# Two attention layers and a post-norm attention in one program: tables made in the first stage, the next weights split inside its last sequence, no wait for the last rows between stages, and the first stage's norm on ScalarE

## What is computed

```python
# stage 1: causal attention, 16 heads of 16, on x [8, 512, 256]; all biases are inputs
q, k, v = split_heads(x @ w_qkv + b_qkv)
a = softmax((q k^T + causal_mask) / sqrt(16))
z = a v
y = z @ w_out + b_out                 # then x + y, normed over its 256 columns
# stage 2, two layers: local attention (8 heads of 64, window 128, l2-normed and rotated q, k), then a gated FFN
for layer in range(2):
    h = shift_token(x); q, k, v = h @ wqkv
    x = x + local_attention(rot(l2norm(q)), rot(l2norm(k)), v) @ wo
    h = layernorm(shift_token(x)) * lg + lb
    a, g = split(h @ w1 + b1)
    x = x + (a * gelu(g)) @ w2 + b2
```

## Time and profile before

| what | value |
| --- | --- |
| median of 3 runs | 2063.98 us (2062.27 to 2068.06) |
| the profiled execution's own time | 2061.79 us |
| its span in the profile | 2060.3 us |
| mean granted TensorE clock | 0.922 of 2.4 GHz |
| TensorE, VectorE, ScalarE, GpSimd busy | 88%, 55%, 46%, 46% of the span |
| first attention | from 7.6 to about 564.9 us |
| local 0 | to 1068.8 us |
| feed-forward 0 | to 1292.7 us |
| local 1 | to 1798.7 us |
| feed-forward 1 | to the end |

### The profile page before, as it was taken

How to read it: one execution, slowest core, us unless ns; L and a number is a source line. 1 busy time by engine, 2 the same in 40 slices (tenths; PEclk the granted TensorE clock), 3 DMA queues, 4 the chain that set the end, 5 groups by cost and what they waited for, 6 DMA issues and landing times. The chain is left out here.

```text
span 2060.3 us, 41179 instructions
## 1 busy us (share of the span) xinstructions
PE 1815.2 (88%) x13304; PEld 1348.1 (65%) x13304; DVE 1141.5 (55%) x2885; ACT 941.3 (46%) x1834; POOL 940.9 (46%) x926
## 2 busy tenths in 40 slices
PE   4899988889569999999969999599999999798887
PEld 2556555655346777777758888467777777577676
DVE  3566665656367766766523333766676666333343
ACT  2555555655335554455434444255445555333322
POOL 3355444554435555554433333355554545333433
PEclk8899888987679999999979999799999999889998
DMA  4333343332210000000111112100000000221221
GB/s 124 107 114 102 102 128 106 120 112 62 72 32 12 31 31 31 31 31 20 48 56 41 61 61 92 43 11 31 31 31 31 31 20 4 79 72 51 81 71 41
DMA packets 103655, 121.27 MB, mean 59 GB/s; under 512 B 23290, under 2 KB 75700, under 8 KB 103604
## 3 DMA queue, kind: packets, MB, share of 16 engines
q1 hardware_dynamic: 96692, 95.45, 15.3%
q0 software_dynamic: 6912, 25.17, 3.3%
HBM read 82.55 MB, written 37.77 MB: 58 GB/s over the span
## 5 line engine op out<-in xcount | busy, mean ns | idle before, releaser
L425 DVE TENSOR_REDUCE a_negm<-a_x 128x2 f32<-128x256 f32 (+3 forms) x256 | 202.5, 815 | 142.1 <-PE a_x L539 139.7
L804 POOL TENSOR_TENSOR work<-work 128x512 f32<-128x512 f32 x128 | 164.7, 1286 | 196.8 <-DVE work L953 195.6
L394 ACT ACTIVATE a_PT<-a_c 128x384 f32<-128x384 f32 (+1 forms) x384 | 184.1, 523 | 138.7 <-PE a_c L578 87.3
L971 DVE CUSTOM_DVE_ANT_0 l_x<-l_x,window 128x256 f32<-128x256 f32 (+1 forms) x512 | 184.4, 422 | 44.7 <-PE l_x L1067 44.0
L1462 DVE SCALAR_TENSOR_TENSOR m_hid<-m_a,mw_b,m_gate 128x512 f32<-128x512 f32 x96 | 71.9, 749 | 246.8 <-ACT m_gate L1401 222.7
L1001 PE MATMUL l_f<-w_hi,tails 128*128 128x512 f32 x384 | 174.9, 455 | 15.0 <-DVE work L953 11.9
L1359 POOL TENSOR_TENSOR m_hid_lo<-m_hid,m_hid_hi 128x512 fp32r<-128x512 f32 x80 | 102.8, 1294 | 134.6 <-ACT m_hid_hi L1412 134.4
L882 ACT ACTIVATE l_PT<-l_c 128x512 f32<-128x512 f32 (+1 forms) x256 | 124.7, 539 | 79.0 <-PE l_c L1103 79.0
L1002 PE MATMUL l_f<-w_hi,tails 128*128 128x512 f32 x384 | 155.3, 405 | 0.0
L1003 PE MATMUL l_f<-w_lo,tails 128*128 128x512 f32 x384 | 154.6, 403 | 0.0
L818 POOL TENSOR_TENSOR l_PS<-l_PT 128x768 f32<-128x768 f32 x64 | 119.7, 1871 | 76.0 <-ACT l_PT L882 76.0
(11 more groups left out here) (238 smaller groups left out, 5115.6 us busy)
## 6 DMA issues: line engine op xcount, KB each, us to landing
a_Q<-qk_parts SPq DMA_DIRECT2D x192, 64.0 KB, 2.1
a_K<-qk_parts SPq DMA_DIRECT2D x192, 64.0 KB, 2.1
qk_parts<-a_qk_hi SPq DMA_DIRECT2D x32, 256.0 KB, 2.1
qk_parts<-a_qk_lo SPq DMA_DIRECT2D x32, 256.0 KB, 2.1
after_attn<-l_out POOLq DMA_DIRECT2D x16, 512.0 KB, 5.8
xin<-after_attn SPq DMA_DIRECT2D x32, 256.0 KB, 3.1
m_xr<-after_attn SPq DMA_DIRECT2D x16, 512.0 KB, 4.1
xin<-in_L_attn_x SPq DMA_DIRECT2D x8, 512.0 KB, 3.5
```

Of the source, the lines that this page charges most:

```text
L394: nc.scalar.activation(PT[:, p // PG % 2, 2 * (p % PG) + hh, QOFF[t]:QOFF[t] + nq], SC[hh][:, 0:nq], ACT.Exp, scale=AD ** -0.5).then_inc(e ...
L425: dve.tensor_reduce(negm[:, q, 2 * p:2 * p + 2], MX[i % 2][:, :, 0:nk], AX.X, ALU.max, negate=True).then_inc(max_done, 1)
L804: pool.tensor_tensor(t1[:, par, w, :], t1[:, par, w, :], t2[:, par, w, :], ALU.add)\
L971: m = dve.tensor_tensor_reduce(out=o, in0=o, in1=mask, scale=-1.0, scalar=-NEG, op0=ALU.add, op1=ALU.min, accum_out=negm[:, q + t, p // 2, ...
```

## The change

1. The constant tables are made at the head of GpSimd's list in `first_attention` (`make_constants`), and the zero rows are set by VectorE there and stored by SyncE in the last sequence. The two blocks ahead of the first attention are gone.
2. At the start, the weights come in two halves with a semaphore each, the four bias columns in two transfers, and the splits of the weights stand behind those of the rows (`f_xe`) on ScalarE and VectorE. `wo_hi` is made after `f_qe:3`, `wo_lo` before `f_sm:4`.
3. In the last sequence of the first attention, SyncE loads the next weights at the first step, ScalarE makes the three high parts after `st:12`, `st:18` and `z3:1`, VectorE the three low parts after `ms:5`, `z0:2` and `z2:3`.
4. The row norm of the first attention (step `end`) runs on ScalarE as scale and bias per row; GpSimd computes the negated mean times the root beside the root, and stores.
5. Stages share one tile `rows_out`. The wait for the eight stores at the end of a stage is gone (but for the last stage); the next stage waits for them (`own.ready`) before it loads sequence 1 or later, before the residual load and before it writes `rows_out`.

The core of the diff:

```diff
+def make_constants(pool, k):
+
+    made = k["made"]
+    pool.memset(k["ident"][:, :], 0.0).then_inc(made, 1)
+    pool.wait_ge(made, 1)
+    pool.affine_select(out=k["ident"][:, :], in_=k["ident"][:, :], compare_op=ALU.not_equal, fill=1.0, base=0,
+                       pattern=[[-1, P]], channel_multiplier=1).then_inc(made, 1)
...
+        HIGH, LOW = [("st", 12), ("st", 18), ("z3", 1)], [("ms", 5), ("z0", 2), ("z2", 3)]
+        FIRST_OF_LAST = [s for s in STEPS if s[0][0] != "f"][0]
...
-                sp.dma_start(w_raw[:, :, :], w_qkv.rearrange("(k p) n -> p k n", p=P)).then_inc(w_loaded, 16)
-                for m, c in enumerate((0, DM, P, DM + P)):
-                    sp.dma_start(bqk[:, m:m + 1], b_qkv[c:c + P].unsqueeze(1),
-                                 allow_slow_non_contiguous=True).then_inc(w_loaded, 16)
+                for k in range(KT):
+                    sp.dma_start(w_raw[:, k, :], w_qkv[P * k:P * k + P]).then_inc(w_loaded[k], 16)
+                for n in range(2):
+                    sp.dma_start(bqk[:, n::2], b_qkv[DM * n:DM * n + DM].rearrange("(h p) -> p h", p=P),
+                                 allow_slow_non_contiguous=True).then_inc(b_loaded, 16)
...
-                steps(sp, do)
-                sp.wait_ge(parts_out, NB * 128)
-                sp.wait_ge(lo_done, NB * 4)
-                ahead.load(sp, ahead_raw, ahead_wo)
-                sp.wait_ge(front_full, NB * NF)
-                sp.wait_ge(stored, 16)
-                ahead.first(sp)
+                def tail(name, i):
+                    if (name, i) == FIRST_OF_LAST:
+                        sp.wait_ge(parts_out, NB * 128)
+                        sp.wait_ge(lo_done, NB * 4)
+                        ahead.load(sp, ahead_raw, ahead_wo)
+                        zeros.store(sp)
+                        sp.wait_ge(front_full, NB * NF)
+                        sp.wait_ge(stored, 16)
+                        ahead.first(sp)
...
                         pool.tensor_scalar(ve[:, :], mv[:, :, 1], LN_EPS, None, ALU.add).then_inc(rstd_a, 1)
-                        pool.wait_ge(rstd_a, b + 2)
+                        pool.tensor_scalar(nb[:, :], mv[:, :, 0], -1.0, None, ALU.mult).then_inc(rstd_a, 1)
+                        pool.wait_ge(rstd_a, 2 * b + 3)
                         pool.tensor_tensor(rs[:, :], ve[:, :], half[:, :], ALU.pow).then_inc(rstd_done, 1)
+                        pool.wait_ge(rstd_done, 2 * b + 1)
+                        pool.tensor_tensor(nb[:, :], nb[:, :], rs[:, :], ALU.mult).then_inc(rstd_done, 1)
                     elif name == "end":
-                        wait_apart(pool, K, rstd_done, b + 1)
-                        wait_apart(pool, K, stored, b * 16)
-                        for t in range(TB):
-                            pool.tensor_scalar(out[:, t, :], y[:, t, :], mv[:, t, 0:1], rs[:, t:t + 1],
-                                               ALU.subtract, ALU.mult).then_inc(out_done, 1)
-                        pool.wait_ge(out_done, b * TB + TB)
+                        wait_apart(pool, K, out_done, b * TB + TB)
                         pool.dma_start(dst[b, 1:1 + S].rearrange("(t p) d -> p t d", p=P),
                                        out[:, :, :]).then_inc(stored, 16)
 
                 steps(pool, do)
-                pool.wait_ge(stored, 16 * NB)
...
+                    elif name == "end":
+                        act.wait_ge(rstd_done, 2 * b + 2)
+                        act.wait_ge(stored, b * 16)
+                        for t in range(TB):
+                            nc.scalar.activation(out[:, t, :], y[:, t, :], ACT.Identity, scale=rs[:, t:t + 1],
+                                                 bias=nb[:, t:t + 1]).then_inc(out_done, 1)
...
+                def tail(name, i):
+
+                    if (name, i) in HIGH:
+                        act.wait_ge(front_full, NB * NF)
+                        ahead.high(act, ahead_raw, ahead_wo, HIGH.index((name, i)))
+
+                steps(act, do, tail)
...
+                def tail(name, i):
+                    if (name, i) in LOW:
+                        ahead.low(dve, ahead_raw, ahead_wo, LOW.index((name, i)))
+
+                steps(dve, do, tail)
...
                         if not isinstance(b, int):
                             sp.wait_ge(front_full, (b - 1) * NF + 2)
+                            sp.wait_ge(own.ready, 16 * NB)
                             sp.dma_start(xin[:, :, :], x[b].rearrange("(t p) d -> p t d", p=P)).then_inc(x_in, 16)
...
                     elif name == "out":
                         dve.wait_ge(xr_in, b * 16 + 16)
+                        dve.wait_ge(own.ready, 16 * NB)
                         dve.wait_ge(stored, b * 16)
```

More of the change, by code:

```diff
@@ L114, in first_attention @@
+def first_attention(nc, K, scr, w, xin, rows_out, zeros, ahead, x, w_qkv, b_qkv, w_out, b_out, dst):
     with ExitStack() as ctx:
@@ L407, in _ @@
                 dve.memset(Q[:, :, S:].bitcast(F32), 0.0).then_inc(v_set, 1)
-                dve.wait_ge(w_split, 2)
-                for kt in range(KT):
-                    dve.tensor_tensor(w_lo[:, kt, :], w_raw[:, kt, :], w_hi[:, kt, :], ALU.subtract)\
-                        .then_inc(w_split, 1)
-                dve.wait_ge(wo_split, 1)
-                dve.tensor_tensor(wo_lo[:, :, :], wo[:, :, :], wo_hi[:, :, :], ALU.subtract).then_inc(wo_split, 1)
+                zeros.set(dve)
                 def do(name, i, b):
@@ L420, in do @@
                                 .then_inc(xlo_done, 1)
+                        if isinstance(b, int):
+                            for kt in range(KT):
+                                dve.wait_ge(w_split, kt + 1)
+                                dve.tensor_tensor(w_lo[:, kt, :], w_raw[:, kt, :], w_hi[:, kt, :], ALU.subtract)\
+                                    .then_inc(w_low, 1)
                     elif name in ("sm", "f_sm"):
@@ L1252, in low, with feed_forward @@
                 .then_inc(self.lo_done, 1)
-def feed_forward(nc, K, lay, own, ahead, x, residual, dst):
+def feed_forward(nc, K, lay, own, ahead, rows_out, x, residual, dst):
     with ExitStack() as ctx:
@@ L1277, in feed_forward @@
         res = sb("res", [P, TB, DM])
-        y, out = sb("y", [P, TB, DM]), sb("out", [P, TB, DM])
+        y, out = sb("y", [P, TB, DM]) if last else rows_out, rows_out
         st2, mv2 = sb("st2", [P, TB, 6]), sb("mv2", [P, TB, 2])
@@ L1292, in feed_forward @@
         w2_done, y_done, xr_in, res_in, stored = (
-            sem("w2_done"), sem("y_done"), sem("xr_in"), sem("res_in"), sem("stored"))
+            sem("w2_done"), sem("y_done"), sem("xr_in"), sem("res_in"), sem("stored") if last else ahead.ready)
         if last:
@@ L1497, in _ @@
                 if ahead is not None:
-                    ahead.low(dve, [ahead_raw[:, k, :] for k in range(KT)], ahead_wo[:, :, :])
+                    for n in range(KT + 1):
+                        ahead.low(dve, [ahead_raw[:, k, :] for k in range(KT)], ahead_wo[:, :, :], n)
             @block.tensor
```

175 lines of the change are left out of this document (94 added, 81 removed).

## The result

| | before | after |
|---|---|---|
| median of the runs, us | 2063.86 (2062.27 to 2068.06, 4 runs) | 2078.69 (2077.06 to 2079.93, 4 runs) |
| profiled execution: own time, span | 2061.79, 2060.3 | 2079.73, 2078.2 |
| mean granted clock of TensorE | 0.922 | 0.912 |

The ratio is 1.0072, interval 1.0057 to 1.0087: slower by 0.7%, 14.8 us. The forecast was 2068.8 and "the same", meant as within 0.3%: that was missed. The time lies within its range, on the slower side, 4 us above the case in which the clock costs 2.4 us a turn and 3 above the one in which the joins do not open.

A forecast was written before the change was run, and what follows sets the result against it. TensorE leads everywhere, so edits count through its waits. Losses of 19.2 (loop) and 8.5 (last sequence) less gains of 22.9 (start, joins) gave +4.8: 2068.8 us, "the same"; own range 2059 to 2076, 8 in 10 within 2055 to 2081.

The forecast's parts named there:

- the case in which the clock costs 2.4 us a turn: Rival for the loop: ScalarE's wait costs TensorE's clock 2.4 instead of 1.4 us every turn, 2074.8 us; chance 0.23.
- the joins do not open: Rival at stage ends: a stage holds until its transfers land, wait or no wait, 2075.5 us; chance 0.07.
- Start, 11.3: Program start: first projection at 9.8 instead of 21.06 us, 11.3 us gained, lower bound 9.5.
- First join, 7.4: End of first attention: store issued 4.9 us earlier, 2.5 less from issue to next stage; 7.4 gained, bounds 4.9 and 8.1.
- Later joins, 4.2: Ends of local 0 and local 1: next stage 0.3 us behind VectorE's end, 2.1 gained each.
- Loop, 3.2 a turn: First attention's loop: 1.8 us of delay plus 1.4 of clock lost per turn, bounds 0 and 4.2; 19.2 over six turns.
- The clock term: Loop, behind the new wait at `st:4`: 3.4 us at 1.2 GHz cost 1.4 us a turn, bounds 0 and 2.4.
- Last sequence, 8.5: First attention's last sequence: stall 4.0, `w_hi` splits 2.8 and `w_lo` 1.7 us, together 8.5 lost, bounds 4 and 10.
- the stall: Last sequence's head: delay of 4.9 us from ScalarE's norm meets only a 0.86 wait before `pv:0`, 4.0 lost.
- its own list: Signs in the profile after; forecast wrong if first score products do not wait for ScalarE, turns keep length or lengthen over 3.5.

The follow-up runs named there:

- experiment 9: Changed kernel with GpSimd's norm in every sequence, next weights' splits at the last one's end, stages waiting for stores again: 2051.7 us, ratio 0.9945.
- experiment 5: Changed kernel with unused products filling three TensorE waits of a turn, ahead of `st:5`, `f_sm:0` and `pv:1`: 2067.6 us, ratio 1.0033.
- experiment 7: Changed kernel with GpSimd's norm in the loop, last stores issued by SyncE and the next weights' early splits undone: 2037.7 us, ratio 0.9880.
- Experiment 2: Kernel before with only the norm moved to ScalarE in all eight sequences, behind the old splits in the last: 2095.2 us, ratio 1.0152.

## Why the prediction was right and wrong

*Start, 11.3.* Right, to 0.1 us at the first projection. At the first `a_ve` the profile shows 7.4, the repeated one 11.5, and nine profiles 9.3 on average; the other 2.0 are lost inside the first sequence, by what is not known. The 11.3 of experiment 9 hold 3.3 from the last sequence, so that they agree with the forecast is luck.

*First join, 7.4.* Measured 5.9. "9.4 us later ... 4.9 earlier" was right (5.0). "Without the wait 0.86 for issuing and the 2.6 remain, 2.5 less" failed: 0.9 was gained. The step took the 2.6 us between landing and next stage as a fixed cost behind the issue. They are not; the wait for landing covered most of what holds a stage's end behind a store of GpSimd's in any case, and this came out from under it.

*Later joins, 4.2.* Failed for the same reason: 0.3 and 0.5. The row that I called evidence against the rival, 0.3 us where the store had landed, was a join whose last store GpSimd had issued 4.5 us before the next stage, as long as such a store holds the end, so it could not tell. The rival "the joins do not open" is what happened, and I gave it 0.07. With the store on SyncE the later joins came out as forecast, at 0.3, and the first one better, 1.56 from issue to next stage where 3.5 was worked out: what the step says of the later joins held for a queue that the kernel did not use.

*Loop, 3.2 a turn.* Measured 4.0. The wait was 4.22 (4 forecast), released by ScalarE, at the place named; the wait for the mask went; TensorE's idle time grew by 0.9 a turn (1.8 forecast). The clock term failed in size: 3.1 where I had 1.4, with 2.4 as the upper bound. Two things were wrong in it. Behind the new wait the clock was low for 6.5 to 7 us and not 3.4, which the term's own working makes 2.7 to 2.9. And the term looked at that one place, while the low stretches of the whole turn changed: with the wait filled they came elsewhere and the turn gained 0.8. The Trainium skill ("TensorE: Matmul & The Clock Gate", "HAM oscillation — how this bites in real kernels") has a kernel's clock fall again and again because of waits. The trace agrees for the new wait of each turn, and differs in experiment 5 and in the kernel before, where the clock also falls behind work with hardly a wait; by the rule alone it had to stay up in experiment 5, for which I had put turns of 58 to 60 us, and they were 63.7.

*Last sequence, 8.5.* Each half holds: the stall cost 3.6 (59.25 less 55.63; 4.0 forecast), the splits 5.0 (4.5 forecast). The profile shows only 5.4 more than before, since a turn with neither part in it is 3.3 us shorter than before: 50.5 in experiment 7 and 50.56 in experiment 9, against 53.9. Experiment 2, with the old splits and the stall, took 57.1, again some 3 more than 50.5 and 3.6. From 17.5 to 23.5 us into it the clock is 1.00 in both, and 0.52 before. What in the change turns the clock there no run tells, and the prediction had no term for it.

*Sum.* By the profiles, up to the start of the first local attention: -7.4 +24.2 +5.4 -5.9 = +16.3; the joins behind it give back 0.8. The remaining 2.4 up to the 17.9 between the two spans lie in stages whose instructions hardly changed, and are no larger than what two executions of one kernel differ by: the second local attention took 506.0, 510.7 and 506.5 us in before, after and its repetition. Against my +4.8, the loop is 5.0 dearer and the joins 4.9 worth less, and that is the move from "the same" to "slower"; 3.9 less from the start and 3.1 less in the last sequence nearly cancel. Two rivals came true together, the clock in size and the joins as a whole; that the time still lies inside the range, 2 us from its end, is owed to the range's width and to that cancelling. It is luck, and no sign that the sum was right. By its own list the forecast was wrong: turns grew by 4.0, over the 3.5 named there, VectorE's last end did not stand 0.3 before the later joins, and the first join opened by 5.9 and not 7.

What stays open: what holds a stage's end after GpSimd's issue (GpSimd itself, or its transfer's landing), what makes the clock fall behind busy stretches, and where the start loses 2 us.

## What to carry to other kernels

An engine's list is a queue: work moved to an engine with time to spare is cheap only at the place where its inputs are ready, and here the same 2.1 us of norm cost 4.0 us a turn at the turn's end and gained 1.8 to 2.9 a turn (61.4 to 59.7 and 58.6) in the middle of the next one. To remove a wait at the end of a stage, look at what ends there anyway: issue the last transfer from the queue that does not hold the stage's end, here SyncE's. And where the clock of TensorE changes within a turn, take a clock term from the mean over whole turns at two kernels, never from one stretch behind one wait.

## What the runs showed of the hardware

- After a store of 512 KB issued by GpSimd, the end of a stage came 4.0 to 5.1 us behind the issue, with the data already at rest for 1.1 to 2.2. Issued by SyncE, it came 1.56 us behind at the first join, with the transfer (2.9 us to landing) still moving.
- The granted clock went to its lower level behind waits of 4.2 and of 1.5 us, and also with TensorE busy for 12.19 of the 13 us ahead, its longest wait being 0.7.
- Less waiting did not mean a higher clock: 43.2 us of idle time in six turns at 0.82, 37.8 at 0.88, 18.5 at 0.84, 10.7 at 0.90.
- The same kernel's first sequence ended at 119.60 and at 115.54 us in two executions, at a mean clock of 0.78 and 0.81; of the 4.1 us, 3.0 are TensorE's busy time and 0.9 its waits.
